# Summing equal targets over pairs of blocks in a graph network kernel, with two scatter waits in each group, another start-up and another order of the node stage

## The reference

```python
h = x @ W_in2f
Wij = ssp(rbf @ Wf1 + bf1) @ Wf2 + bf2
Wij = Wij * dist_cut                      # edge_weight1
x_ij = h[idx_j] * Wij                     # idx_j = dst
m = segment_sum(x_ij, idx_i, n_atoms)     # idx_i = src
m = ssp(m @ Wo1 + bo1) @ Wo2 + bo2
out = layernorm(x + (x + m))
```

## Time and profile before

| | us |
|---|---|
| median of 3 runs (2079.63 to 2088.7) | 2085.95 |
| the profiled execution's time | 2090.3 |
| its span, first to last instruction | 2088.5 |

### The profile page before, as it was taken

One profiled execution on the slowest core, in us unless ns is written; L12 is line 12 of the kernel. 1 busy time (PEld: TensorE's weight loads), 2 busy tenths in 40 slices (PEclk: granted clock), 3 DMA queues, 4 the chain that ended last, 5 costly groups with the idle time before them and its releaser, 6 DMA issues. The chain is left out here.

```text
span 2088.5 us, 37484 instructions
## 1 busy us (share of the span) xinstructions
PE 1886.3 (90%) x11780; PEld 1606.7 (77%) x11780; DVE 1637.4 (78%) x3663; ACT 1550.2 (74%) x3137; POOL 1535.3 (74%) x1384
## 2 busy tenths in 40 slices
PE   1899999999999999999999898895999999999997
PEld 1788888888888888888887787784777777777775
DVE  2788888888888888888888877783677777777774
ACT  0777888778787787887787776672777777777775
POOL 5422788888888888888888888763677777777776
PEclk9999999999999999999999999996999999999997
DMA  6999566666666666666666666664577777777762
GB/s 204 388 396 388 106 113 120 118 118 112 112 118 119 118 116 109 117 119 117 119 112 112 120 110 119 105 151 98 192 255 254 248 251 253 252 248 253 255 241 104
DMA packets 265299, 363.33 MB, mean 174 GB/s; under 512 B 125848, under 2 KB 177261, under 8 KB 265104
## 3 DMA queue, kind: packets, MB, share of 16 engines
q0 software_dynamic: 75136, 102.45, 29.6%
q1 hardware_dynamic: 72724, 207.27, 28.1%
q10 hardware_dynamic: 117244, 51.22, 10.5%
HBM read 206.71 MB, written 154.12 MB: 173 GB/s over the span
## 5 line engine op out<-in xcount | busy, mean ns | idle before, releaser
L333 POOL DMA_INDIRECT acc<-sums,src_ix x392 | 652.0, 1663 | 142.0 <-issue 111.3
L320 POOL DMA_INDIRECT xg<-in_x,dst_t x392 | 414.7, 1058 | 226.9 <-PE pair L403 106.8
L363 POOL TENSOR_SCALAR sums<-sums,neg_mean,rstd 128x256 f32<-128x256 f32 x392 | 349.1, 904 | 10.2
L478 PE MATMUL pair<-m_h,same 128*128 128x256 f32 (+1 forms) x980 | 253.6, 295 | 50.9 <-ACT sums L607 50.9
L719 DVE SCALAR_TENSOR_TENSOR same<-srcb,src_t,later 128x512 fp32r<-128x512 int32 (+3 forms) x392 | 289.9, 800 | 0.0
L509 PE MATMUL pair<-wo_h,ssp_h 128*128 128x256 f32 (+1 forms) x784 | 264.8, 338 | 0.0
L755 DVE SCALAR_TENSOR_TENSOR m_l<-pair,wgt_t,m_h 128x256 fp32r<-128x256 f32 x392 | 171.7, 480 | 107.2 <-ACT m_h L600 107.2
L478 PEld LDWEIGHTS pair<-m_h,same 128*128 128x128 f32 (+1 forms) x980 | 183.9, 188 | 89.0 <-issue 86.6
L478 PE MATMUL pair<-m_l,same 128*128 128x256 f32 (+1 forms) x980 | 238.3, 279 | 0.0
L392 PE MATMUL pair<-wo_h,msg_h 128*128 128x256 f32 (+1 forms) x784 | 229.8, 293 | 3.3 <-DVE m_l L755 2.8
L509 PE MATMUL pair<-wo_h,ssp_l 128*128 128x256 f32 (+1 forms) x784 | 224.5, 286 | 0.0
(11 more groups left out here) (105 smaller groups left out, 5375.3 us busy)
## 6 DMA issues: line engine op xcount, KB each, us to landing
acc<-fill SPq DMA_DIRECT2D x195, 256.0 KB
xg<-in_x SPq DMA_DIRECT2D x97, 512.0 KB, 4.3
sums<-acc SPq DMA_DIRECT2D x97, 512.0 KB, 4.2
out<-sums SPq DMA_DIRECT2D x97, 512.0 KB, 2.9
attr<-in_edge_attr ACTq DMA_DIRECT2D x194, 128.0 KB, 4.6
srcb<-in_src ACTq DMA_DIRECT2D x97, 256.0 KB, 4.3
xg<-in_x,dst_t POOLq DMA_INDIRECT x392, 3.7
acc<-sums,src_ix POOLq DMA_INDIRECT x392
```

Source lines behind the costliest of these rows:

```text
L320: pool.indirect_dma_start(xg[0:g.p, g.xs, r], None, t["x"], bass.IndirectOffsetOnAxis(ap=dst_t[0:g.p, r, g.n:g.n + 1], axis=0)).then_inc(x ...
L333: pool.indirect_dma_start(acc, bass.IndirectOffsetOnAxis(ap=src_ix[g.slot][0:g.p, r:r + 1], axis=0), sums[0:g.p, g.slot, r], None, compute ...
L363: last = pool.tensor_scalar(normed[0:g.p, g.n % NRING, r], res[0:g.p, u, r], neg_mean[0:g.p, u, r:r + 1], rstd[0:g.p, u, r:r + 1], ALU.add ...
L478: last = pe.matmul(o, same[0:g.p, g.par, FROM[a] + b - a, 0:g.p], m[0:g.p, a], start=a == 0 and m is m_h, stop=a == b and m is m_l)
```

## The change

- **Sums over pairs.** `compare` and `summed` take blocks 0 and 1 together and blocks 2 and 3 together: 6 of 10 block pairs, 12 of 20 matmuls. Targets can now be equal between the two pairs of a group, so the third scatter of a group waits for the first two (`added`) as the first one waits for the previous group; gathers are issued between the pairs too. AHEAD goes from 21 to 20 groups.
- **Start-up.** The tables of the first 96 groups are loaded as 96 rows and turned by TensorE; those of the last two groups come separately. Weights and biases are loaded on ACT's queue, split by ACT and VectorE between the first groups' stages, and waited for only where first used. ACT's group loads move to SP, where they alternate with the clears (24 first, then 15 a step).
- **Node stage.** `cap_2` is gone (the logarithm adds 0.5 as its bias, the maximum caps it at 40); one of four squared deviations moves from ACT to VectorE; TensorE does both transposes of a group ahead of the output products of an earlier one; the bo2 product has 128 partitions, all but two of them zero; x is fetched as its buffers come free at the end of the edge stage.

```diff
-AHEAD = 21
+AHEAD = 20
+FIRST_CLEARS = 24
+CLEARS_A_STEP = 15
...
+    MAIN = G - G % 16
...
-        FROM = [0, 4, 7, 9]
-        same = sb("same", [P, 2, R * (R + 1) // 2, P], F32R)
+        FROM = [0, 2, 3, 5]
+        same = sb("same", [P, 2, 6, P], F32R)
...
+            for n in range(2, G + 1):
+                if n < G:
+                    load_attr(n)
+                load_src(n - 1)
+                clear_to(FIRST_CLEARS + (n - 1) * CLEARS_A_STEP)
...
-            for n in range(XRING):
-                fetch_x(group(n))
+            for n in range(G - XRING, G):
+                fetch_x(group(n % XRING))
...
                         pool.wait_ge(src_ready, g.n + 1)
-                        wait(pool, added, g.n * R * 16)
                     if r % 2 == 0:
+                        wait(pool, added, (g.n * R + r) * 16)
                         pool.wait_ge(y_sb, g.n * 2 + r // 2 + 1)
...
                 for r in range(R):
                     scatter(r)(group(n))
+                    if r == 1:
+                        gather_to(AHEAD * R + (2 * n + 1) * (G - AHEAD) * R // (2 * (G - 4)))
                 gather_to(AHEAD * R + (n + 1) * (G - AHEAD) * R // (G - 4))
...
-                        for a in range(b + 1):
+                        for a in range(2 * q, b + 1):
...
-            run((turn2(0), 0), (out2(0), 2), (turn2(1), 0), (out2(1), 2))
+            run((turn2(0), 0), (turn2(1), 0), (out2(0), 2), (out2(1), 2))
...
-                act.activation(z, z, ACT.Ln).then_inc(ln2, 1)
+                act.activation(z, z, ACT.Ln, bias=half[:]).then_inc(ln2, 1)
...
-                for r in range(R):
+                for r in range(R - 1):
...
-                dve.tensor_tensor(ssp2[g.par][:].rearrange("m h n -> m (h n)"), pair[g.par][:].rearrange("m h n -> m (h n)"),
-                                  grown[g.par][:].rearrange("m h n -> m (h n)"), ALU.max).then_inc(ssp2_sb, 1)
+                dve.scalar_tensor_tensor(out=ssp2[g.par][:].rearrange("m h n -> m (h n)"), in0=grown[g.par][:].rearrange("m h n -> m (h n)"), scalar=LN_MAX,
+                                         in1=pair[g.par][:].rearrange("m h n -> m (h n)"), op0=ALU.min, op1=ALU.max).then_inc(ssp2_sb, 1)
...
+                dve.scalar_tensor_tensor(out=squares[0:g.p, R], in0=res[0:g.p, u, r], scalar=neg_mean[0:g.p, u, r:r + 1], in1=res[0:g.p, u, r],
+                                         op0=ALU.add, op1=ALU.mult, accum_out=square[0:g.p, u, r:r + 1]).then_inc(square_dve, 1)
...
-            run((cap_2, 0), (ssp2_low, 1), (softplus_2, 0), (residual, 2))
+            run((ssp2_low, 1), (deviation_last, 3), (softplus_2, 0), (residual, 2))
```

289 lines of the change are left out of this document (171 added, 118 removed).

## The result

| | before | after |
|---|---|---|
| median, us (runs) | 2087.32 (4) | 1979.11 (4, 1967.62 to 1982.55) |
| the profiled execution: time, span | 2090.3, 2088.5 | 1967.62, 1965.9 |

A forecast was written before the change was run, and what follows sets the result against it. The prediction took GpSimd to bound the edge stage, with TensorE close. First scatter 184, edge groups 1340, tail 50, node stage 514 and 1.8 around the span gave 2090 us; the 8-in-10 range was 2010 to 2190.

The forecast's parts named there:

- GpSimd sets the edge stage: Edge stage: GpSimd never rests, 12.52 us a group before and 14.26 after; a TensorE saving alone buys nothing.
- The mean gap of 3.5 us: Edge stage: mean wait on GpSimd between scatter pairs, two a group, from 3.0 us without edge loads and 4.2 with.
- 0.45 of the gaps: Edge stage: share of gaps in which edge loads meet a scatter's landing, (4.5 + 2.0) / 14.3.
- Rival C: Edge stage: loads meet a gap in nearly every group, mean gap 4.2 us, 15.66 a group, 2222 in all; chance 0.16.
- Rival B: Edge stage: gathers cover the landing, mean gap 3.1 us, 13.46 a group, 2015 in all; chance 0.24.
- B2: Edge stage: landings as short as the last, 2.0 + 0.3 us, mean gap 2.7, 1938 us in all; chance 0.04.
- an estimate of 2.6 us for a gap: Edge stage: from the skill page's fixed 2.0 us and bytes over 436 GB/s, 2.3 us for 128 KB.
- The start at 184: Start-up: first scatter at 184 us in place of 216.4, bounds 175 and 195, gain 32 us.
- The bytes are the same: Start-up: clears interleaved with group loads move the same bytes on full engines, so they still take 165 us.
- The node stage at 4.9 us: Node stage: a group takes 4.9 us in place of 6.29, GpSimd and transfers close together; bounds 4.6 and 5.4.
- TensorE's 4.3: Node stage: TensorE's time a group in us if the bias product hides as the others do; 5.0 at most.
- The bias product's price: Node stage: 0.38 us for the bias product on 2 partitions; four products of 1.22 us, 0.98 each were all alike.

The follow-up runs named there:

- e1: The kernel before with the edge-stage part alone (sums over pairs, second wait, gathers between the pairs, 20 groups ahead): 2168.8 us, 1.0415 of before.
- e2: The changed kernel with sums over all four blocks again and one wait a group: 1908.2 us, 0.9149 of before.
- e4: The changed kernel without the edge_attr loads after the third group (stale attributes): 1939.6 us.
- e10: The changed kernel with the node stage's bias product on 2 partitions again, as in the kernel before: 2122.1 us, 1.0077 of before.
- e6: The changed kernel with three of four blocks normalised on GpSimd in the node stage: 2000.3 us.
- e7: The changed kernel with two of ScalarE's three squared deviations in the node stage: 1977.9 us.
- e3: The changed kernel with all gathers of a group behind its fourth scatter, none between the pairs: 2178.2 us, 1.0444 of before.

## Why the prediction was wrong

- **GpSimd sets the edge stage: right.** e1 is slower with fewer matmuls, e2 faster with more, and the tail came to 49.8 us against 50. Its arithmetic holds as well: 4 x 1.65 + 2 x 0.30 + 2 x 3.09 = 13.4 us, 13.45 measured.
- **The mean gap of 3.5 us: the step that failed in the edge stage,** by its share and not by its sizes. A landing with no load in it took 3.0 us as assumed (3.06 and 2.82 in the table), one with a load 4.26 against 4.2. But 0.45 of the gaps were charged with a load, from (4.5 + 2.0) / 14.3, as if the loads came at random. They don't: most went out 0.5 to 1.0 us after the end, where the gaps are short; 29 of 187 gaps, 0.16, were late (0.13 to 0.25 in the seven profiles, mean gap 3.09 to 3.26). 2 x 0.41 x 94 = 77 us. Rival C argued from this very rhythm, for a loss; it was the rhythm, with the other sign. Rival B had the right edge stage (13.46 us a group, 1265 us), against the chance of 0.24 that it was given, and its argument ("the gathers cover the landing") was the right one. That its 3.1 us came out so closely is luck: the measured mean is made of gaps of 2.71 to 3.27, late ones included.
- **B2 was half right.** The bare gap inside a group has a median of 2.54 us and a least of 2.42; that between groups a median of 3.01. In the tail of after, where no load goes out behind 1464.27, the gaps from 1479 on are 2.52 (inside), 2.94 (between), 3.89, 3.00 and 2.41 us. The 3.89 is a late landing with no load near, which stays open. The two kinds of bare gap (start, duration, idle time before):

```profile
1499.37 1.49 POOL L364 DMA_INDIRECT acc<-sums,src_ix  x1 [3.00 <-issue]
...
1505.04 1.48 POOL L364 DMA_INDIRECT acc<-sums,src_ix  x1 [2.41 <-DMA acc<-sums,src_ix]
...
1510.22 1.75 SPq L304 DMA_DIRECT2D sums<-acc  x4
```

  The Trainium skill ("DMA: Bandwidth & Descriptors", section "Anatomy of one DMA — SWDGE (gpsimd) path"), by which the prediction had worked out an estimate of 2.6 us for a gap, fits the inner gap's 2.41 to 2.54 and not the outer one's 3.0. The half microsecond between them isn't in the landing. By the semaphore events the landing comes 2.26 us after the end of the pair in both (medians of the gaps with one gather that aren't late); the next scatter starts 0.27 us behind that inside a group and 0.72 us between groups, where it also waits for the group's targets. Whether that wait is the cause was not tried.
- **The start at 184: short by 12 us.** The clears began at 9.2, earlier than the 14.4 forecast, but went out until 191.1, 182 us and not 165:

```profile
L287 SPq DMA_DIRECT2D acc<-fill x195: 427/642/1655, 9.2 to 191.1; - x195
```

  "The bytes are the same" was the wrong step. TensorE starts its groups 35 us earlier than before (17.35 against 52.35), and between the first and the last clear there are 78 gathers in place of 63; the group loads there are 36 in place of 38. In all 68.5 MB move in that stretch in place of 64.2, at 377 GB/s in place of 389, and the two together make up the 17 us. In e4, without the edge_attr loads, it is 65.5 MB at 390 GB/s; the clears take 168 us (9.1 to 177.0) and the scatters begin at 183.2.
- **The node stage at 4.9 us: the step that failed there; it is 4.37 us,** from exp to exp, as the 6.29 before it. The value was GpSimd's sum of 5.0, made from rows in which four normalisations took 3.62 us. That was a duration beside busy neighbours, not a cost: the four took 904 ns each before, 740 in the node stage after, 559 in e10 and, three of them, 978 in e6. It was the one term of five (4.4, 4.4, 4.3 to 5.0, 4.43, 4.9) that could give way, and it was chosen because it was the largest. What holds at last is ScalarE, put at 4.4, with VectorE and TensorE just behind. TensorE's 4.3, named in the prediction for the case "if the bias product hides as the others do", is near what came true (4.25 in e7, with TensorE full), though the prediction's own rows give 4 x 0.84 + 1.1 = 4.5 for that case. The Trainium skill's rule of shared interfaces ("GPSIMD Engine Reference", section 8 "Key points") was to add 0.2 us on GpSimd, at most 0.5. Durations do vary so in the rows (978 ns; 349 against 170), though no run separates the cause, and in after the group's pace is ScalarE's all the same.
- **The bias product's price** was seen as 0.38 us in the rows and its removal as 1.22 - 0.98 = 0.24 us a product; it was 0.33 (e10), and it decides the stage.
- **The sum.** The two stages' errors have the same sign, and so the measured median lies 31 us below a range of 180 us. The range had been built on rivals that change one term at a time; B together with the node stage's lower bound of 4.6 would have given 2015 - 29 = 1986, and 1979 was measured.

## What to carry to other kernels

The cost of a wait for a DMA's landing can depend on when other loads go out: look in the trace for their place against the end of the instruction waited for, before charging them by their share of the time. An instruction's duration beside busy neighbours is no lower bound for its engine; take the pace of a stage from the engine whose work can't shrink. And a matmul on 2 partitions isn't small: ask what it does to those behind it.

Two parts of a change with opposite signs hide each other: without the pairs the same kernel is at 0.9149 of before, against 0.9475 with them.

## What the runs showed of the hardware

- A scatter-add of 128 rows of 1 KB lands 2.3 us after the end of its instruction (median), and releases the next one 2.3 to 2.4 us after that end at best (2.29 in e4, 2.42 in after). Where loads went out between 3.0 us before and 0.5 us after the end, the next one started 4.1 to 4.3 us after it on the mean (60 of 64 late in e3, 14 of 14 in after), and the landing came after 3.9. With loads 0.5 to 1.0 us after the end no gap was late (48 of 48 in after).
- A bias product on 2 of 128 partitions costs 0.33 us more for each product group than on 128, with the other 126 partitions zero (e10 against after). It starts 206 ns after the product ahead of it in place of 118, its weight load only with it, and the next product 308 ns later in place of 118.
- GpSimd's normalisation of one block takes 559 to 978 ns, and VectorE's 128 x 4 multiplication 170 to 349 ns, by what runs beside them.
- The granted clock was 0.93 in the edge stage after, where TensorE waits for gathers, against 0.99 before. No run shows that it cost time there, where GpSimd was the bound.
